# A recommendation tower in streams of 64 samples, with one gathered table, a base buffer of its own and an unrolled program

## The reference, cut to what matters

```
# 1024 samples; 32 ids each, one table per field; rows of 16
e = stack([tbl_f[ids[:, f]] for f in range(32)], axis=1)        # (1024, 32, 16)
x0 = xk = e
for W in (W0, W1, W2):                                           # (32, hk, 64)
    xk = relu(einsum('bmd,bhd,mhk->bkd', x0, xk, W))             # three layers of 64 maps
    outs.append(sum(xk, axis=2))                                 # sum over d
h = concatenate([*outs, dense_ctx], axis=1)                      # (1024, 208)
h = maximum(h @ W_top1 + b_top1, 0); h = maximum(h @ W_top2 + b_top2, 0)
y = h @ W_top3                                                   # (1024, 1)
```

## Time and profile before

| | us |
|---|---|
| median of three runs | 689.96 (688.97 to 692.24) |
| span of the profiled execution, first to last instruction | 769.5 |
| busy in it: TensorE matmul, VectorE, GpSimd, ScalarE | 609.3, 577.9, 469.8, 236.9 |
| moved by DMA | 149.77 MB |
| mean granted TensorE clock | 0.918 |

### The profile page before, as it was taken

How to read it: one execution, slowest core, us unless ns; L and a number is a source line. 1 busy time by engine, 2 the same in 40 slices (tenths; PEclk the granted TensorE clock), 3 DMA queues, 4 the chain that set the end, 5 groups by cost and what they waited for, 6 DMA issues and landing times.

```text
span 769.5 us, 8172 instructions
## 1 busy us (share of the span) xinstructions
PE 609.3 (79%) x2818; PEld 219.3 (28%) x2818; DVE 577.9 (75%) x292; ACT 236.9 (31%) x440; POOL 469.8 (61%) x362
## 2 busy tenths in 40 slices
PE   0265179949996699939996499996997399999998
PEld 0121023313331134303332133322332133333334
DVE  0003199949994699849995599985995499999994
ACT  0022144206331154306431063425331063325331
POOL 6757447845797168853897258945897248704630
PEclk9978579979998699969999699998999599999999
DMA  5059800699039940699019950499329950399300
GB/s 169 7 154 373 306 1 1 226 356 366 21 124 327 363 153 4 193 393 361 19 41 333 377 214 5 146 342 373 104 56 337 358 215 6 105 376 372 105 1 0
DMA packets 58834, 149.77 MB, mean 195 GB/s; under 512 B 10728, under 2 KB 24048, under 8 KB 58816
## 3 DMA queue, kind: packets, MB, share of 16 engines
q1 hardware_dynamic: 50624, 147.42, 52.2%
q0 software_dynamic: 8192, 2.11, 4.2%
HBM read 145.30 MB, written 4.20 MB: 194 GB/s over the span
## 4 chain that ended last, share of the span: by engine, by line
PE 49%; another core or an unknown queue 16%; DVE 13%; issue 12%; ACT 5%; DMA 3%; POOL 1%; SPq 1%; DVEq 0%; ACTq 0%; POOLq 0%
PE acc L695 42%; DVE zd L509 11%; DMA rolled<-x_scratch 2%; DVE zpart L481 2%; ACT xk_ps L558 2%; PE mlp L743 2%; ACT xk_sb L558 2%; POOL emb L402 1%; PE acc L704 1%; POOL zg L414 1%; ACT relu_ab L564 1%; PE xk_ps L774 1%; PE mlp L735 1%; DMA z2d<-dense_t_in 1%
## 5 line engine op out<-in xcount | busy, mean ns | idle before, releaser
L509 DVE TENSOR_TENSOR zd<-rolled,xk_ps 128x2048 f32<-128x2048 f32 x240 | 533.7, 2278 | 134.6 <-issue 51.4
L695 PE MATMUL acc<-zd,w_sb 128*64 128x512 f32 x1664 | 399.5, 615 | 95.4 <-DVE zd L509 62.2
L414 POOL TENSOR_TENSOR zg<-rolled,xk_sb 128x1024 f32<-128x1024 f32 x96 | 225.8, 2379 | 174.8 <-ACT xk_sb L558 148.3
L402 POOL DMA_INDIRECT emb<-tbl_in,ids_tile x192 | 182.3, 949 | 69.6 <-issue 68.2
L695 PEld LDWEIGHTS acc<-zd,w_sb 128*64 128x64 f32 x1664 | 117.1, 140 | 341.2 <-issue 218.2
L558 ACT ACTIVATE xk_ps<-acc 64x512 f32<-64x512 f32 x128 | 73.0, 570 | 210.1 <-PE acc L695 122.9
L564 ACT ACTIVATE relu_ab<-acc 128x512 f32<-128x512 f32 x48 | 28.7, 597 | 259.5 <-PE acc L695 237.2
L695 PE MATMUL acc<-zg,w_sb 128*64 128x512 f32 x384 | 100.1, 601 | 2.4 <-POOL zg L414 2.4
L695 PE MATMUL acc<-zd,w 128*64 128x512 f32 x256 | 65.1, 636 | 18.0 <-issue 11.2
L402 POOL DMA_INDIRECT emb<-tbl_in,ids_sb x64 | 60.6, 946 | 27.1 <-issue 24.9
L558 ACT ACTIVATE xk_sb<-acc 64x512 f32<-64x512 f32 x128 | 75.7, 591 | 3.1
(11 more groups left out here) (74 smaller groups left out, 149.4 us busy)
## 6 DMA issues: line engine op xcount, KB each, us to landing
rolled<-x_scratch SPq DMA_DIRECT2D x252, 512.0 KB
xk_sb<-x_scratch SPq DMA_DIRECT2D x15, 512.0 KB
x_scratch<-x0t SPq DMA_DIRECT2D x16, 256.0 KB
emb<-tbl_in,ids_tile POOLq DMA_INDIRECT x192
emb<-tbl_in,ids_sb POOLq DMA_INDIRECT x64
w_sb<-w_in SPq DMA_DIRECT2D x2, 512.0 KB
zg<-select_in SPq DMA_DIRECT2D x1, 640.0 KB
wt<-wtop_in SPq DMA_DIRECT2D x1, 512.0 KB
```

Source lines behind the costliest of these rows:

```text
L402: pool.indirect_dma_start(emb[:, f * DIM:(f + 1) * DIM], None, tables[f], bass.IndirectOffsetOnAxis(index[:, f:f + 1].bitcast(U32), 0)).th ...
L414: nc.gpsimd.tensor_tensor(zg[:, plan_of(t).slot("pool", n), :], rolled[:, j, s * STREAM:(s + 1) * STREAM], xk_sb[:, s, :], ALU.mult).then_ ...
L509: nc.vector.tensor_tensor(zd[:, plan_of(t).slot("dve", n), 0:w, :], rolled[:, j:j + w, s * STREAM:(s + 1) * STREAM], twice(xk_ps[:, s, :], ...
L695: last = nc.tensor.matmul(acc[h * MAPS:(h + 1) * MAPS, s, :], weights, z[:, h * HALF:(h + 1) * HALF], start=(i == 0 and c == 0), stop=(i = ...
```

## The change

The streams are cut by samples in place of d: a stream is 64 samples by 16 d, again 1024 columns; there are 16 streams (`STREAMS`), still in pairs a and b (even and odd) of one 128-sample tile. The 32 tables become one table of 757,000 rows, with the first row of each field added to the ids on VectorE. Fields lie on partitions: partition 4f + g holds field f and samples 16g to 16g+15 of the stream, so a stream takes 16 gathers of 128 rows, and the landed tile is already in the order of the scratch. The transposes, `x0t` and its copy are gone, and so are the head's transposes and selections. The scratch has a place for each stream. The base lands in a buffer `base` of its own and is squared from there into `xk_sb`. The chunks of a stream are all loaded together, in the merged order in which the third layer of the stream two before frees them, and the store of stream b stands in the middle of the loads of stream a. The dense inputs are loaded once and y is stored once. All programs are written out, with no loop. Tile 0 has another order of phases.

```diff
+ORDER = [(0, 0), (0, 1), (1, 0), (0, 2), (1, 1), (1, 2)]
+for _t in range(1, TILES):
+    ORDER += [(2 * _t + s, layer) for layer in range(3) for s in range(2)]
+POOL_CHUNKS = {(0, 0): 0, (1, 0): 0, (0, 1): 4, (1, 1): 2, (0, 2): 4, (1, 2): 2}
+GATHERS_BEFORE = 8
+GATHERS_AFTER = [1, 1, 1, 1, 5, 5, 1, 1, 1, 1, 2, 2]
+GATHERS_LEAD = 8
...
+            def store_scratch(i):
+                sp.wait_ge(gathered[i % 2], 16 * GATHERS * (i // 2 + 1))
...
+            def load_stream(i):
+                s = i % 2
+                sp.wait_ge(scratch_in[s], 32 * (i // 2 + 1))
+                if i > 0:
+                    sp.wait_ge(base_ps, 2 * i)
+                    sp.wait_ge(squares_ready, i)
+                sp.dma_start(base[:, :], rows_from(0, i, 0)).then_inc(base_in, 16)
+                order = PLAN.merged[phase_of(i - 2, 2) if i > 1 else phase_of(i, 1)]
+                for k, (who, n, first, w) in enumerate(order):
+                    if i > 1:
+                        sp.wait_ge(zd_ready if who == "dve" else zg_ready, n + 1)
+                    for j in range(first, first + w):
+                        sp.dma_start(rolled[:, s, j, :], rows_from(BASES[j], i, 1)).then_inc(rolled_in[s][j], 16)
+                    if k == len(order) // 2 and s == 0 and i > 0:
+                        store_scratch(i + 1)
...
+            store_scratch(0)
+            load_stream(0)
             store_scratch(1)
+            load_stream(1)
+            for t in range(1, TILES):
+                store_scratch(2 * t)
+                load_stream(2 * t)
+                load_stream(2 * t + 1)
...
+            total = STREAMS * GATHERS
+            pool.wait_ge(first_index, 1)
+            for g in range(2 * GATHERS):
+                gather(g)
+            done = 2 * GATHERS
+            for t in range(TILES):
+                for g in range(done, min(total, done + GATHERS_BEFORE + (GATHERS_LEAD if t == 0 else 0))):
+                    gather(g)
+                    done = g + 1
+                place = 0
+                for q in range(6 * t, 6 * t + 6):
+                    if PLAN.pool[q]:
+                        pool.wait_ge(xk_sb_ready, 4 * evacuations(before_in_slot(q)))
+                    for _, n, j, _ in PLAN.pool[q]:
+                        product(q, n, j)
+                        for g in range(done, min(total, done + GATHERS_AFTER[place])):
+                            gather(g)
+                            done = g + 1
+                        place += 1
...
                 nc.vector.tensor_reduce(zpart[:, t % 2, layer, s, :],
-                                        relu_ab[:, s, :].rearrange("p (d b) -> p b d", b=TB),
+                                        relu_ab[:, s, :].rearrange("p (b d) -> p b d", d=DIM),
...
+            def base_to_ps(i):
+                s = i % 2
+                act.wait_ge(base_in, 16 * (i + 1))
                 for h in range(2):
                     nc.scalar.copy(xk_ps[:, s, h * HALF:(h + 1) * HALF],
+                                   base[:, h * HALF:(h + 1) * HALF]).then_inc(base_ps, 1)
+                nc.scalar.activation(xk_sb[:, s, :], base[:, :], ACT.Square).then_inc(squares_ready, 1)
...
+            for t in range(1, TILES):
+                evacuate(q)
...
+                evacuate(q + 5)
+                if not last:
+                    base_to_ps(2 * t + 3)
```

More of the change, by code:

```diff
@@ L65, with __init__ @@
+GATHERS_BEFORE = 8
+GATHERS_AFTER = [1, 1, 1, 1, 5, 5, 1, 1, 1, 1, 2, 2]
+GATHERS_LEAD = 8
 class Plan:
-    def __init__(self, pool_chunks, like=None, pool_last=()):
-        self.phases = []
+    def __init__(self):
+        self.dve, self.pool, self.merged = [], [], []
         nd = ng = 0
-        for p, (_, layer) in enumerate(PHASES):
+        for stream, layer in ORDER:
             n = L0CH if layer == 0 else NCH
[L78 to L81, removed]
+            split = n - POOL_CHUNKS[stream % 2, layer]
+            dve = [("dve", nd + i, j, min(2, split - j)) for i, j in enumerate(range(0, split, 2))]
+            pool = [("pool", ng + i, j, 1) for i, j in enumerate(range(split, n))]
+            merged, taken = [], 0
@@ L88, in __init__ @@
+            self.pool.append(pool)
+            self.merged.append(merged + pool[taken:])
             nd += len(dve)
             ng += len(pool)
[L90 to L98, removed]
@@ L133, in build_cin_tower, with phase_of, before_in_slot, evacuations @@
-def build_cin_tower(nc, ids, dense_t, tables, w0a, w0b, w0c, w12, wtop1, btop1, wtop2, btop2, wtop3,
-                    eye, eye2, select, out):
+PLAN = Plan()
+def phase_of(stream, layer):
+    return ORDER.index((stream, layer))
+def before_in_slot(q):
+    same = [x for x in range(q) if ORDER[x][0] % 2 == ORDER[q][0] % 2]
+    return same[-1] if same else None
+def evacuations(q):
+    return sum(layer < 2 for _, layer in ORDER[:q + 1])
+def build_cin_tower(nc, ids, dense_t, tables, w0a, w0b, w12, wtop1, btop1, wtop2, btop2, wtop3, eye, out):
@@ L801, in _ @@
-            tile(0)
-            with pe.Fori(1, TILES - 2) as t:
-                tile(t)
-            tile(TILES - 2)
-            tile(TILES - 1, ahead=False)
+            for q in range(6):
+                phase(q)
+            for t in range(1, TILES):
+                q = 6 * t
+                phase(q)
+                phase(q + 1)
+                zsum(t - 1)
+                phase(q + 2)
+                mlp1(t - 1)
+                phase(q + 3)
+                mlp2(t - 1)
+                phase(q + 4)
+                mlp3(t - 1)
+                if t == TILES - 1:
+                    pe.wait_ge(reduced, q + 4)
+                    half_sums(t, stage[0:MAPS, 0:TB], 0)
+                    half_sums(t, stage[MAPS:P, 0:TB], 1).then_inc(last_z01_done, 1)
+                phase(q + 5)
@@ L880 @@
     out = nc.dram_tensor("y_out", (BATCH, 1), F32, kind="ExternalOutput").ap()
[L881 to L882 removed]
+    build_cin_tower(nc, out=out, **aps)
     r = run_bass_kernel_spmd(nc, [arrays], core_ids=[0])
```

660 lines of the change are left out of this document (209 added, 451 removed).

## The result

| | before | after |
|---|---|---|
| median, us | 690.63 (688.97 to 692.24, 4 runs) | 699.14 (697.87 to 699.42, 4 runs) |
| ratio after / before | | 1.0123, 95% interval 1.0082 to 1.0164 |
| span of the profiled execution | 769.5 | 697.3 (its own time 699.1) |

The change makes the kernel 1.2% slower. 719 was forecast, and a range of 676 to 742, which holds the result. But 719 was 29 above the median known then (689.96), and only 8.5 came.

The account below looks back on a forecast made before the run. VectorE and TensorE were taken to bound a tile, with late gathers delaying stream b after the change. 151.5 (head) + 469.7 (six tiles) + 5 (restarts) + 71.7 (tail) = 697.9, plus 21.6 for holes: 719 us, range 676 to 742.

Parts of the forecast that it names:

- the closed-up sum: Whole kernel with the holes closed up: 646.7 us before, 697.9 after, 51.2 above before.
- Phase (0,2): Head, tile 0: held behind phase (0,1) and ScalarE's evacuation, it starts on VectorE at 81.5 us, on GpSimd at 83.9.
- S1: Start of VectorE's phase 2 in tile 1: 143 us before, 151.5 after, so the head loses 8.5.
- S to S: Six tiles between starts of VectorE's phase 2: late gathers delay stream b, 469.7 us against 430.5, 39.2 lost.
- Tail: From the last S to the end: five cheaper sums bring 73.2 us to 71.7.
- The sum over d: VectorE's 48 sums of 128x512: contiguous reads and fewer results bring 1.04 us each to 0.69.
- half-speed restarts: TensorE restarts at half speed after each of five holds in the tiles: 1.0 us each, 5 in all.
- The written-out program: More code is fetched, claimed to cost nothing; upper bound a hole like the 14.95 us in a tile.
- the 1.25 of a gather: GpSimd's gather spacing in us, kept beside VectorE's work against a skill rule that would make gathers far dearer.
- the 43.3: Median of the runs before above the closed-up time, in us, taken as holes at tile borders; half, 21.6, carried over.
- rival D: Loads in the order of freeing do what they say and stream b is in time: 668 us, chance 0.07.
- Rival B: At the tile borders the late stream swallows all holes: 697.9 us, slower by 1.1%, chance 0.11.

Follow-up runs that it names:

- a_storeend: Kernel after with the store of stream b issued behind all chunk loads of stream a, not in their middle: 674.10 us, ratio to before 0.9775.
- a_gather10: Kernel after with 10 gathers ahead of each tile's products instead of 8, on chip 10: 713.89 us, ratio to before 0.9278.
- b_noburst: Kernel before without its 18 gathers at the tile border (old rows for 18 fields in tiles 2 to 7), chip 10: 703.06 us, ratio 0.9129.
- after_third: Kernel after, unchanged, run on chip 12: 724.86 us, the kernel before 767.64, ratio 0.9455.
- b_shallow: Kernel before with at most six loads under way: 768.63 us, ratio 0.9965.
- a_pause: Kernel after with store at end, phase (0,1) by VectorE alone, 10 gathers ahead, extra gathers held until VectorE's tenth pair: 654.82 us, ratio 0.9447.

## Why the prediction was wrong, step by step

**Right: the closed-up sum.** It gave 697.9; the profiled span is 697.3. First product 34.5, measured 35.45. GpSimd's first product 63.0, measured 62.78. Phase (0,2) on VectorE 81.5, measured 81.01; (1,2) 126.1, measured 126.74. S1 151.5, measured 153.05. S to S 70.7, 75.6, 77.1, 79.6, 82.1, 84.6, measured 73.8, 74.1, 77.5, 79.4, 82.9, 84.2. Tail 71.7, measured 72.3. The sum over d was taken at 0.69 and is 0.678. Small misses partly cancel, which is luck: S1 came 1.5 late and the tail 0.6, while the tiles, with the 5 us of half-speed restarts, were to take 474.7 and took 471.9. a_storeend shows the mechanism by taking 25.0 us off with one line, and a_gather10 by taking SyncE's standing before its stores from 266.6 to 48.9.

**Right: the code.** The written-out program cost nothing that shows: no wait of VectorE in the six tiles ends by issue in the session of the result.

**Two readings in it.** From 57.5 to 606.1 us the timeline has 14 waits of VectorE over 2 us, 113.2 in all, not 12 and 108.5; nothing in the sum rests on it. And the price set against the 1.25 of a gather is that of a copy by VectorE, while VectorE makes products here: the rows neither bear it out nor contradict it.

**Wrong: the 43.3.** The failed step is this: "the runs hold about a third of the holes, or what lies around the span", and half of it, 21.6, was carried over to the kernel after. What lies around the span is 1.6 to 1.8 us. It was not in the sum at all. The rest I had taken for the holes of the profile, made smaller, and they are not. The profiled execution of 769.5 belongs to the group above 762, the timed runs to that below 699. In an execution of the second group S1 is 143.5 (closed up: 143), the tail 73.6 (73.2), and all 41.7 us lie in the six tiles, with no wait of VectorE ended by issue or remote. Nine times there TensorE waits over 1 us for a chunk of GpSimd, 28.7 us in all; in six of them, 20.2 us, GpSimd's product had itself waited over 1 us for its load. In the kernel before these are the last chunks of a stream in its load order and the first that GpSimd wants. In the kernel after, whose loads follow the order in which chunks are used and freed, GpSimd waits for no load at all in the list of waits: 118.9 us for `xk_sb` and 8.1 for a slot. So there was nothing to carry: 719.5 - 699.1 is 20.4, that is 21.6 too much for holes, 0.6 too much in the closed-up sum and 1.8 too little around the span. The change did what rival D said of its loads, and gave it back in the same place: six tiles of 472.2 before and 471.9 after. What remains are the head, 153.05 - 143.5 = 9.5 lost, and the tail, 1.3 won; with the 0.3 of the tiles that is 7.9, and 8.0 lie between the two spans (697.3 - 689.3).

How the rest of the 41.7 splits is not shown: in the other three of the nine waits GpSimd had stood behind its own gathers or waited for `xk_sb`. And a kernel with the old order of loads and all else of the change was not run, so that the new order is what removed them is argued from the list of waits. Rival B had the right time, 697.9, with another mechanism: nothing was swallowed.

**Not foreseen: the sign changes with the chip.** On chip 12 the spans are 762.7 and 722.2. Of the 40.5, 10.8 lie before S1 and 29.5 in the six tiles: there the kernel before pays where its 18 gathers meet the loads (b_noburst), and the one after, with at most 10 in a row at a border, pays less. That the shorter bursts are the reason is not shown: no run on chip 10 or 12 changed the bursts alone. The late gathers cost the same 84.2 in the last tile on both chips.

## What to carry to other kernels

Before a hole in a profile is scaled down to fit a shorter median, ask whether that execution and the timed ones are of one kind; if they differ by more than the runs among themselves, the shorter ones may wait for something else altogether. In a queue that runs in order, a store that waits for a late producer belongs behind all that does not need it: one line was worth 25.0 us here. A steady state needs its supply to equal its use (30 gathers a tile for 32 used made a wait that grew from 2.1 to 13.5 us in five tiles), and work done ahead of time (48 gathers before a first product) must not stand in front of what the next engine waits for.

## What the runs showed of the hardware

**On some chips engines start late where gathers meet loads.** The head of the kernel after, timeline of ScalarE, then of TensorE, first on chip 12 (after_third), then in the first session (after):

```profile
69.49 2.35 ACT L381 ACTIVATE xk_ps<-acc 64x512 f32<-64x512 f32 x4 [37.26 <-issue]
```

```profile
42.02 1.90 PE L475 MATMUL acc<-zd,w 128*64 128x512 f32 x8
74.98 1.97 PE L475 MATMUL acc<-zd,w_sb 128*64 128x512 f32 x4 [31.07 <-ACT relu_ab L388]
```

```profile
44.78 2.36 ACT L381 ACTIVATE xk_ps<-acc 64x512 f32<-64x512 f32 x4 [12.36 <-PE acc L475]
```

```profile
42.84 1.90 PE L475 MATMUL acc<-zd,w 128*64 128x512 f32 x8
50.27 1.12 PE L475 MATMUL acc<-zd,w_sb 128*64 128x512 f32 x2 [5.53 <-ACT relu_ab L388]
```

And windows of the same stretch (PE, PEld, DVE, ACT, POOL busy, granted clock, DMA share, GB/s), again chip 12 first:

```profile
43.00:62.00 19.00, 0.91 (x6) 0.03 (x2) 0.00 (x0) 0.00 (x0) 14.34 (x16) 0.63 0.88 297
```

```profile
43.00:62.00 19.00, 8.37 (x26) 2.02 (x20) 11.86 (x6) 7.34 (x12) 14.41 (x16) 0.76 0.86 295
```

In both TensorE is done with its last matmul of the phase by 45. ScalarE's evacuation waits for that matmul alone by the program; it starts at 44.78 in the one and at 69.49 in the other. In between the DMAs move the same 295 and 297 GB/s, and GpSimd issues the same 16 instructions. Code being fetched is not the reason: no packet of an instruction queue moves on chip 12 from 44.0 to 69.5, and none in the first profile of the kernel before from 231 to 618, while five of its borders have their hole. The last gather ends at 62.8, and ScalarE starts 7 us later. In the kernel before the holes of 6 to 15 us at the borders end by issue or remote too, and go for the most part with the 18 gathers (b_noburst); the depth of the load queue does not matter (b_shallow).

**There the trace also lacks records.** From 42.5 to 62.0 it holds 463 updates of semaphores in the one and 27 in the other, one each 0.7 us whatever their source. That is not the pace at which signals arrived, for the missing ones do not come later: the whole trace of this program has 10,659 updates in the one and 7,036 in the other, with the same DMA packets to within one. All profiles divide alike: 10,537 to 10,659 where the time belongs to the lower group, 5,471 to 7,096 where it belongs to the upper one. A wait whose releasing update is missing is put down to issue or remote, as ScalarE's is above. So in the earlier trace rows these two words do not name a cause, and the late starts and the missing records come together without a run that shows which brings the other.

**How much it is worth** goes by the kernel: 77 us for the kernel before (767.6 and 691.1), 26 for the one after (724.9 and 699.1).

**What stays open** is why the chips differ, whether the hole of the head ends with the gathers (a_pause ran where there is none), and whether the recording of the events takes part in it, since every execution here was recorded and records are missing where it is slow. The Trainium skill, "NOTIFIC — Programmer's Manual", section "When the ring fills", says that a queue of such records can be set to drop new ones, to overwrite old ones or to stall the engine that makes them. No run here shows which of these was set, and none was made without records.

**TensorE's clock** on chip 12 was granted at 0.63 of full speed on average from 43 to 62, where TensorE was idle but for the first 0.9 us, at 0.50 from 75 to 77, and at 1.00 in the full stretch of the earlier trace rows; its matmuls at 74.98, behind the wait, run at the lower of its two levels, 1.2 in place of 2.4 GHz (1.97 for a chunk, 1.03 in the earlier trace rows).
